# Cross-attention kernel, two layers: the row d goes to all partitions by two small DMAs instead of by TensorE and ScalarE, with a new steady order on all engines

## The reference

```python
q = einsum('bte,ef->btf', emb, Wq) + bq
k = einsum('bml,le->bme', latent, Wk) + bk
v = einsum('bml,le->bme', latent, Wv) + bv
w = softmax(einsum('bte,bme->btm', q, k) / sqrt(512), axis=1)   # over t
x = einsum('btm,bme->bte', w, v) + emb
out = (x - mean(x)) * rsqrt(var(x) + 1e-6) * gamma + beta       # over e
```

## Time and profile before

| | |
|---|---|
| median of 3 runs | 1019.43 us (1016.87 to 1020.06) |
| profiled execution, own time | 1016.79 us |
| its span, first to last instruction | 1014.9 us |
| granted TensorE clock, mean | 0.995 |
| busy: TensorE / its weight loads | 989.6 us (98%) / 930.9 us (92%) |
| busy: VectorE / ScalarE / GpSimd | 876.8 (86%) / 664.1 (65%) / 567.6 (56%) us |
| DMA | 98.32 MB in 373,958 packets, 97 GB/s |

### The profile page before, as it was taken

One profiled execution on the slowest core, in us unless ns is written; L12 is line 12 of the kernel. 1 busy time (PEld: TensorE's weight loads), 2 busy tenths in 40 slices (PEclk: granted clock), 3 DMA queues, 4 the chain that ended last, 5 costly groups with the idle time before them and its releaser, 6 DMA issues. The chain is left out here.

```text
span 1014.9 us, 23859 instructions
## 1 busy us (share of the span) xinstructions
PE 989.6 (98%) x6940; PEld 930.9 (92%) x6940; DVE 876.8 (86%) x2616; ACT 664.1 (65%) x1864; POOL 567.6 (56%) x522
## 2 busy tenths in 40 slices
PE   7989999999999999999999999999999999999985
PEld 6879999999999999999999999999999999999975
DVE  4788889988988998888988988898898889888867
ACT  2457767666766666776766676677667666667642
POOL 0134575556566555656555556655565665556574
PEclk9999999999999999999999999999999999999998
DMA  8653434544444454443454444345444445544101
GB/s 213 134 113 77 104 80 97 109 99 102 101 98 78 100 113 98 97 99 84 90 108 97 105 99 98 79 97 114 97 97 100 90 87 105 115 96 97 54 19 37
DMA packets 373958, 98.32 MB, mean 97 GB/s; under 512 B 308488, under 2 KB 357786, under 8 KB 373914
## 3 DMA queue, kind: packets, MB, share of 16 engines
q1 hardware_dynamic: 371370, 96.98, 44.2%
q10 hardware_dynamic: 2544, 0.80, 0.4%
HBM read 83.06 MB, written 14.68 MB: 96 GB/s over the span
## 5 line engine op out<-in xcount | busy, mean ns | idle before, releaser
L680 PE MATMUL oq_bank<-probs,raw 125*128 125x224 f32 x1488 | 302.8, 353 | 1.7 <-ACT probs L929 1.7
L680 PEld LDWEIGHTS oq_bank<-probs,raw 125*128 125x128 f32 x1488 | 272.2, 190 | 2.3 <-ACT probs L929 1.2
L913 ACT ACTIVATE probs<-probs,neg_max 125x224 f32<-125x224 f32 x378 | 177.8, 472 | 143.7 <-DVE neg_max L1194 143.6
L1521 POOL TENSOR_TENSOR psum<-probs 125x672 f32<-125x672 f32 x62 | 100.1, 1615 | 243.8 <-ACT probs L929 243.8
L656 PE MATMUL score_bank<-qT_hi,cT_hi 128*125 128x224 f32 x768 | 199.6, 286 | 3.9 <-ACT cT_hi L870 1.8
L657 PE MATMUL score_bank<-qT_hi,cT_lo 128*125 128x224 f32 x768 | 188.9, 273 | 0.0
L929 ACT ACTIVATE probs<-probs,rsum 125x224 f32<-125x224 f32 x378 | 150.8, 471 | 10.8 <-DVE rsum L1210 9.4
L1584 POOL TENSOR_TENSOR y_out<-z,gamma_row 112x512 f32<-112x512 f32 x62 | 93.9, 1536 | 113.9 <-ACT z L953 113.9
L656 PEld LDWEIGHTS score_bank<-qT_hi,cT_hi 128*125 128x125 f32 x768 | 145.2, 189 | 8.8 <-ACT cT_hi L870 3.4
L661 PE MATMUL score_bank<-qT_lo,cT_hi 128*125 128x224 f32 x768 | 147.1, 273 | 0.0
L657 PEld LDWEIGHTS score_bank<-qT_hi,cT_lo 128*125 128x125 f32 x768 | 145.4, 189 | 0.0
(11 more groups left out here) (136 smaller groups left out, 2038.9 us busy)
## 6 DMA issues: line engine op xcount, KB each, us to landing
raw<-in_ctx_dram SPq DMA_DIRECT2D x64, 375.0 KB
cb<-in_ctx_dram SPq DMA_DIRECT2D x248, 92.0 KB
x<-in_x_dram SPq DMA_DIRECT2D x32, 448.0 KB, 3.6
xb<-in_x_dram SPq DMA_DIRECT2D x124, 112.0 KB, 3.0
out_dram<-y_out SPq DMA_DIRECT2D x31, 448.0 KB, 6.7
cb<-in_ctx_dram SPq DMA_DIRECT2D x124, 3.5 KB
y<-in_L_xattn_Wq_dram SPq DMA_DIRECT2D x2, 512.0 KB, 5.5
Wq_next<-in_L_xattn_Wq_dram SPq DMA_DIRECT2D x2, 512.0 KB, 12.6
```

The costliest lines, as they stand in the source:

```text
L680: ins = nc.tensor.matmul(o, raw[0:MP, u.slot, c, cols], probs[0:MP, u.par4, c, :], start=(c == 0), stop=(c == MC - 1))
L913: ins = act.activation(probs[0:MP, u.par4, c, :], probs[0:MP, u.par4, c, :], ACT.Exp, bias=neg_max[0:MP, u.par4, c:c + 1], scale=-1.0, acc ...
```

## The change

- **d.** `save_d` (ScalarE's queue) writes the two columns of d_col to a DRAM tensor d_kept[2, 224], and `spread_d`, now on ScalarE's queue too, reads it back broadcast to 125 partitions of d_row. d_col, d_row and d_kept have two copies by layer, with semaphores d_saved and d_done of each. The layer-0 units a0 and a1 of the opening still go over TensorE and ScalarE (`first_spread_d`, `first_d_out`). save_d waits for both dots and for the spread of the same layer before it; spread_d waits for save_d's transfer and for the score_max of two units before.
- **Waits.** transpose_x no longer waits for d_out, dot waits for the saving of two units before.
- **Order.** The steady turns of all engines are written anew, with other offsets of the units; the opening ends earlier and the first turn takes over its rest.
- **SyncE.** A turn was load_cb(a), load_xb, load_x, load_ctx l = 0, load_ctx l = 1, store. It is load_xb, store, load_x, load_ctx l = 0, load_cb of the next batch, load_ctx l = 1.

```diff
-        d_col = sb("d_col", [P, TH])
-        d_row = sb("d_row", [P, T])
+        d_col = sb("d_col", [P, 2, TH])
+        d_row = sb("d_row", [P, 2, T])
...
+        d_kept = nc.dram_tensor("d_kept", [2, T], F32, kind="Internal").ap()
...
             def turn(i, j):
                 a, b = units(i, j)
-                if a(+0).later(1):
-                    load_cb(a(+0))
                 if a(+1).later(1):
                     load_xb(a(+1))
+                store(b(-2))
                 if a(+1).later(1):
                     load_x(a(+1))
                 if a(+0).later(0):
                     load_ctx(a(+0), 0)
+                if a(+1).later(1):
+                    load_cb(a(+1))
+                if a(+0).later(0):
                     load_ctx(a(+0), 1)
-                store(b(-2))
...
+            def save_d(u):
+
+                if not u.real:
+                    return
+                if u.past(-2):
+
+                    act.wait_ge(d_done[u.layer], u.batch(16))
+                act.wait_ge(dot_done, u.n(m=2))
+                act.sem_inc(wait_alone, 1)
+                act.dma_start(d_kept[u.par].rearrange("(h p) -> p h", h=TH), d_col[0:TP, u.par, :],
+                              allow_slow_non_contiguous=True).then_inc(d_saved[u.layer], 16)
+
+            def spread_d(u):
+
+                if not u.real:
+                    return
+                if u.past(-2):
+
+                    act.wait_ge(smax_done, u.n(-2, 6))
+                act.wait_ge(d_saved[u.layer], u.batch(16, 16))
+                act.sem_inc(wait_alone, 1)
+                act.dma_start(d_row[0:MP, u.par, :], d_kept[u.par].partition_broadcast(MP)).then_inc(d_done[u.layer], 16)
```

TensorE's steady turn, whole:

```diff
             def turn(i, j):
                 a, b = units(i, j)
+                o_product(b(-2), 0)
+                score_product(a(-1), 2)
+                transpose_x(b(-1), 0)
+                o_product(b(-2), 1)
+                transpose_x(b(-1), 1)
+                pv_product(b(-2), 0)
+                q_product(b(-1), 0)
+                pv_product(b(-2), 1)
+                q_product(b(-1), 1)
+                o_product(a(-1), 0)
+                score_product(b(-1), 0)
+                score_product(b(-1), 1)
+                o_product(a(-1), 1)
+                score_product(b(-1), 2)
+                pv_product(a(-1), 0)
+                q_product(a(+0), 0)
+                q_product(a(+0), 1)
+                pv_product(a(-1), 1)
                 score_product(a(+0), 0)
-                o_product(b(-1), 1)
-                transpose_x(b(+0), 0)
                 score_product(a(+0), 1)
-                score_product(a(+0), 2)
-                transpose_x(b(+0), 1)
-                pv_product(b(-1), 0)
-                q_product(b(+0), 0)
-                pv_product(b(-1), 1)
-                q_product(b(+0), 1)
-                o_product(a(+0), 0)
-                spread_d(b(+0))
-                score_product(b(+0), 0)
-                score_product(b(+0), 1)
-                o_product(a(+0), 1)
-                score_product(b(+0), 2)
-                q_product(a(+1), 0)
-                pv_product(a(+0), 0)
-                spread_d(a(+1))
-                pv_product(a(+0), 1)
-                q_product(a(+1), 1)
-                o_product(b(+0), 0)
```

More of the change, by code:

```diff
@@ L580, in transpose_x @@
                     pe.wait_ge(z_done, u.n(-UNIT_GAP, 2))
[L581 to L582 removed]
+                if g == 0 and u.first:
+                    pe.wait_ge(d_done[0], 16 * 2)
+                elif g == 0:
+                    pe.wait_ge(xT_lo_done, u.n(-2, 2))
                 else:
@@ L764, in opening @@
                 spread_bq(1)
-                spread_d(a1)
+                first_spread_d(a1)
                 score_product(a1, 0)
                 spread_bk(1)
-                transpose_x(b0, 0)
                 score_product(a1, 1)
[L770 to L780, removed]
-                pe.wait_ge(c_done, (LC + 1) * LAYERS)
[L783 to L787, removed]
+                pe.wait_ge(c_done, (LC + 1) * LAYERS)
             opening()
@@ L962, in turn @@
                     standardise(a(-2), 1)
-                ctxT_hi(a(-1), 3)
+                o_hi(b(-2), 0)
+                exps(a(-1), 0)
+                xT_hi_part(b(-1), 0)
+                save_d(b(-1))
                 o_hi(b(-2), 1)
-                xT_hi_part(b(-1), 0)
-                exps(a(-1), 0)
                 xT_hi_part(b(-1), 1)
+                exps(a(-1), 1)
                 xT_hi_part(a(+0), 0)
-                exps(a(-1), 1)
+                normalise(a(-1), 0)
                 q_hi(b(-1), 0)
-                normalise(a(-1), 0)
                 normalise(a(-1), 1)
+                spread_d(b(-1))
                 q_hi(b(-1), 1)
@@ L976, in turn @@
                 xT_hi_part(a(+0), 1)
+                save_d(a(+0))
                 o_hi(a(-1), 0)
-                d_out(b(-1))
-                exps(b(-1), 0)
+                ctxT_hi(a(+0), 0)
+                ctxT_hi(a(+0), 1)
                 o_hi(a(-1), 1)
@@ L982, in turn @@
                 standardise(b(-2), 1)
-                ctxT_hi(a(+0), 0)
+                spread_d(a(+0))
+                exps(b(-1), 0)
+                ctxT_hi(a(+0), 2)
                 q_hi(a(+0), 0)
+                q_hi(a(+0), 1)
+                exps(b(-1), 1)
                 normalise(b(-1), 0)
-                exps(b(-1), 1)
-                normalise(b(-1), 1)
-                q_hi(a(+0), 1)
-                ctxT_hi(a(+0), 1)
-                o_hi(b(-1), 0)
             WkT_out(0)
@@ new lines, in turn @@
+                q_lo(b(-1), 0)
+                add_pv(b(-2), 0)
+                xT_lo_part(a(+0), 0)
+                half_moments(b(-2), 0)
+                q_lo(b(-1), 1)
+                if j is None and i == 2:
+                    Wv_lo_part(1)
+                turn_x(a(+0), 1)
+                moments(b(-2), 0)
+                add_pv(b(-2), 1)
+                xT_lo_part(a(+0), 1)
+                turn_ctx(a(+0), 0)
+                half_moments(b(-2), 1)
+                ctxT_lo(a(+0), 0)
```

188 lines of the change are left out of this document (78 added, 110 removed).

## The result

| | before | after |
|---|---|---|
| median of the runs, us | 1018.8 (1016.9 to 1020.1) | 1454.7 (1445.6 to 1459.8) |
| profiled execution: its own time, its span, us | 1016.8, 1014.9 | 1453.6, 1451.8 |
| TensorE busy, share of the span | 989.6 us, 98% | 1073.0 us, 74% |
| distance of two loads of raw, l = 0, in one turn | 29.81 us | 44.08 us |

The ratio is 1.427, with a 95% interval of 1.4232 to 1.4309. The forecast was 1044 us, in a range of 1004 to 1080. Slower was right; the size was not.

The account below looks back on a forecast made before the run. The prediction took TensorE's instruction stream as the bound. From 1016.8 it took 12.4 and added 34.8 for stalls on raw and 3.8 for the opening: 1043.0, or 1045.7 on the median, stated as 1044 us, range 1004 to 1080.

Parts of the forecast that it names:

- Bound: TensorE, busy all 120.00 us of the middle, sets the steady time; what leaves it is gained in full unless something arrives late.
- Part 1: TensorE loses two spread_d a turn and some returns from float32: 0.4 us a turn, 12.4 us over 31 turns.
- Part 2: ScalarE swaps two d_row copies for two DMA issues and waits; VectorE's work is reordered; costed at nothing if transfers come in time.
- rival 4: d late: at 8 us a transfer, ScalarE and VectorE each about 1 us late every turn; 1038 us, chance 0.05.
- Part 3: SyncE's order: raw's second half behind cb takes 16.3 us against TensorE's 15.1; stall 1.2 us a turn, 34.8 us.
- rival 3: SyncE's cb issues held up by the load in front: 12.26 us, stall 3.9, 1121 us; chance 0.07 including all above 1080.
- The 3.8 us of the opening: In the opening, the second batch's raw loads stand behind cb, ready at 76.7 where o_product started at 72.94: 3.8 us.
- The 12 to 13 us: Sign expected on SyncE's timeline: the second load of raw issued 12 to 13 us after o_product(b, 0) ends.
- The rule ahead of the rivals: Skill page's DMA formula, 2.0 us plus bytes over 436 GB/s: raw's load takes 2.9 us, chain 13.5 us, no stall.

Follow-up runs that it names:

- experiment 2: Changed kernel without its d transfers, with float32 products nobody reads put ahead of TensorE's wait for raw: 1220.63 us with 30, 1130.93 us with 14.
- experiment 6: Kernel before, spread_d(a(+1)) moved to the end of TensorE's turn: 1018.41 us; then also b's transposes placed around o_product(b(-1), 1): 1091.59 us.
- experiment 1: Changed kernel with ScalarE's two d transfers replaced by semaphore increments, most units using an old d: 1201.13 us (1.1771).

## Why the prediction was wrong, step by step

- **Bound: right.** Nothing waited in front of TensorE, and all that came late was lost in full.
- **Part 1, -12.4 us: about half of it shown.** The turns of experiment 2 give back some 0.2 us, not 0.4. The 0.07 for a return from float32 is not confirmed by experiment 6.
- **Part 2, the d transfers at nothing: the step that failed most, 254 us of the 411 missed.** I asked whether the transfers come in time for those who read them, and so did rival 4 with 8 us each. The saves land in 8.9 by the page of after, near that price, and ScalarE waits 40 to 80 us in all, of which 9 reach TensorE. But the cost lies with others: the loads of raw and cb, on another queue, come late while 224 pieces of 4 bytes are written. I had costed the transfer by its bytes and by its reader, and not by its pieces and its neighbours.
- **Part 3, the chain: mechanism right, sizes short.** Without the d transfers, from issue to issue of raw it takes 11.9 us, not 10.2 (0.28 + 0.4 + 9.5); the load takes 6.8, not 5.7; the stall is 3.7, not 1.2. The first difference is the issues of cb directly behind a load of raw: 3.20 for two that take 0.94 when free. That was in the earlier trace rows, 3.11 at 89.36, and I had set it aside as rival 3, because two loads were queued there and not one. One is enough. That rival 3's stall of 3.9 is nearly what came is in part luck: it had 12.26 for cb, where 11.1 came (492.00 to 503.08), and left the load at 5.7. The 3.8 us of the opening didn't come: experiment 1 has no wait on raw there. The 12 to 13 us that the prediction gives for the second load of raw behind the end of o_product(b, 0) don't follow from its sum either, which makes them 10.6; 12.4 came.
- **A term that was missing: the clock.** Rival 3 gave 1121 for that stall, and the order takes 1201. 70 us of the 80 between are the granted clock of 0.50 behind each wait (experiment 2). The steady turns of before couldn't show it, since TensorE never waited there, but its opening does, at 0.50 behind a wait of 1.80 us with little work around it:

```profile
55.09 0.34 PE L656 MATMUL score_bank<-qT_hi,cT_hi 128*125 128x224 f32 x1 [1.80 <-ACT cT_hi L870]
...
56.00:58.00 2.00, 2.00 (x11) 2.00 (x11) 2.00 (x5) 0.74 (x2) 0.00 (x0) 0.50 0.36 101
```

The term could have been bounded from that: o_product at half the clock, 2.3 us more a turn.
- **Rival 4, part of what it said of the place:** VectorE does come late, but on cb (236 us), not on d_row (3.4).
- **The rule ahead of the rivals,** by which the load would take 2.9 us, is farther off than before: 6.8 in experiment 1.
- **The whole turn of after:** 44.08 - 29.81 = 14.3 us. The stall of 11.61, 1.94 for o_product at the low clock (4.21 instead of 2.27), less 0.4, are 13.2. The last 1.1 were not traced.

## What to carry to other kernels

Price a DMA by its pieces and their size at the target as well as by its reader: who else is in flight while it is, and what do they wait for? Where a change gives a full engine its first regular wait, add to the wait what the clock takes behind it. And where a row shows the cost that you are about to argue away, keep it in the range until an experiment has removed it.

## What the runs showed of the hardware

- 4-byte pieces into DRAM: 64 saves of 896 bytes (224 pieces each) cost 302 us in the kernel before, and landed in 8.4 us; pieces of 512 bytes, or SBUF as the target, cost 0.8 and 1.4 us, no more than the noise, and landed in 3.3 and 3.9.
- Two issues of cb behind a load of 375 KB on the same queue take about 3 us instead of 0.9, and one such load in front is enough.
- Beside these small writes, SyncE's 371,370 packets take 573 us of the 16 DMA engines' time instead of 449.
- TensorE's granted clock, 1.00 when a wait began, was 0.79 in 518 to 522 of after and 0.50 in the 4.6 us behind the 3.7 us wait of experiment 1. With 14 small products in that wait it stayed at 1.00. The Trainium skill, TensorE: Matmul & The Clock Gate, section on the HAM clock gate, has the rate as one of two and set by how busy the engine has lately been; the rows agree: 0.50 is the lower one, and 0.79 the mean of a stretch in which it fell.
